# A decoder block with a mixture of experts: plain float32 down products for two of four batches, the router's weight parts side by side, and other orders on every engine

## The reference

```python
x = _layernorm(x + _L0_attn_ref(x, ...))             # a diagonal complex recurrence over the tokens
x = _layernorm(x + _L0_xattn_ref(x, fside, ctx))     # a gated product per batch, with int8 quantization
x = _layernorm(x + _L0_ffn_ref(x, gup, dp, router))  # 8 experts of width 176, the best 2 of each token
```

```python
logits = h @ router_w.T
probs = jax.nn.softmax(logits.astype(jnp.float32), axis=-1)
vals, idx = lax.top_k(probs, TOP_K)
vals = vals / vals.sum(axis=-1, keepdims=True)
combine = jnp.zeros((T, E)).at[jnp.arange(T)[:, None], idx].add(vals)
def step(acc, per_expert):
    gup, dp, cw = per_expert
    gate, up = jnp.split(h @ gup.T, 2, axis=-1)
    y = jax.nn.silu(gate) * up @ dp.T
    return (acc + cw[:, None] * y, None)
```

## Time and profile before

| | |
|---|---|
| median of 3 runs | 167.23 us (167.18, 167.23 and one of 250.56) |
| the profiled execution | 168.11 us |
| its span, first to last instruction | 166.3 us |
| PE busy | 91% |
| DVE, ACT, POOL busy | 71%, 52%, 50% |
| PE clock granted, mean | 0.987 of full |

### The profile page before, as it was taken

The page is one execution under the profiler, slowest core; times in us unless marked ns, Lnnn a source line. Parts: engine busy times, 40 slices in busy tenths (PEclk is TensorE's granted clock), DMA queues, the critical chain, the costliest instruction groups (busy, mean ns, idle before and its releaser), DMA issues.

```text
span 166.3 us, 3462 instructions
## 1 busy us (share of the span) xinstructions
PE 150.7 (91%) x1186; PEld 143.0 (86%) x1186; DVE 118.6 (71%) x395; ACT 86.0 (52%) x185; POOL 83.5 (50%) x131
## 2 busy tenths in 40 slices
PE   7599888976995999999999999999999999999980
PEld 7399666865794999899989999998999999999980
DVE  3992999989889898797998958854837725254432
ACT  7330589687872687552776645456246131522401
POOL 4710599896975039534265453323494312646412
PEclk9959999999999999999999999999999999999998
DMA  4999970000000285000444000175200015510001
GB/s 117 274 409 399 360 247 2 0 0 2 4 2 0 31 165 151 5 4 2 140 145 99 0 0 0 49 148 139 88 0 0 32 36 166 146 42 0 0 32 63
DMA packets 13313, 14.55 MB, mean 87 GB/s; under 512 B 1744, under 2 KB 13040, under 8 KB 13040
## 3 DMA queue, kind: packets, MB, share of 16 engines
q1 hardware_dynamic: 13296, 14.34, 29.1%
HBM read 13.25 MB, written 1.08 MB: 86 GB/s over the span
## 4 chain that ended last, share of the span: by engine, by line
PE 64%; DVE 16%; DMA 6%; POOL 4%; issue 3%; SPq 3%; ACT 2%; POOLq 0%; DVEq 0%; ACTq 0%
PE ps_gu L350 10%; PE ps_gu L351 10%; PE ps_gu L355 10%; PE ps_out L371 5%; PE ps_out L375 5%; PE ps_out L372 5%; DMA u_feat<-in_xT 3%; DMA gu_raw<-share_rows 2%; PE ps_gu L530 2%; DVE one_hot L1552 2%; PE ps_ab L389 1%; POOL gu_raw L1179 1%; POOL rs L1136 1%; SPq L276 1%; PE ps_ab L485 1%
## 5 line engine op out<-in xcount | busy, mean ns | idle before, releaser
L350 PE MATMUL ps_gu<-x_hi,gu_hi 128*128 128x256 f32 x176 | 47.3, 291 | 0.0
L1179 POOL TENSOR_TENSOR gu_raw<-gu_raw 128x512 f32<-128x512 f32 (+1 forms) x24 | 30.7, 1290 | 31.9 <-DVE gu_raw L1573 23.5
L351 PE MATMUL ps_gu<-x_hi,gu_lo 128*128 128x256 f32 x176 | 45.6, 282 | 0.0
L355 PE MATMUL ps_gu<-x_lo,gu_hi 128*128 128x256 f32 x176 | 35.2, 282 | 0.0
L350 PEld LDWEIGHTS ps_gu<-x_hi,gu_hi 128*128 128x128 f32 x176 | 33.1, 188 | 0.2
L351 PEld LDWEIGHTS ps_gu<-x_hi,gu_lo 128*128 128x128 f32 x176 | 33.2, 189 | 0.0
L355 PEld LDWEIGHTS ps_gu<-x_lo,gu_hi 128*128 128x128 f32 x176 | 27.0, 188 | 0.0
L1579 DVE TENSOR_TENSOR hid_lo<-gu_raw,hid_hi 128x512 fp32r<-128x512 f32 (+1 forms) x24 | 17.4, 733 | 8.9 <-ACT hid_hi L806 8.8
L1573 DVE TENSOR_TENSOR gu_raw<-sil,ps_gu 128x512 f32<-128x512 f32 (+1 forms) x24 | 15.2, 638 | 8.2 <-PE ps_gu L355 5.5
L371 PE MATMUL ps_out<-dp_hi,hid_hi 128*128 128x256 f32 x77 | 20.6, 288 | 0.3 <-DVE u_feat L1587 0.2
L788 ACT ACTIVATE sil<-ps_gu 128x512 f32<-128x512 f32 (+1 forms) x24 | 13.3, 555 | 12.8 <-PE ps_gu L355 12.7
(11 more groups left out here) (272 smaller groups left out, 318.7 us busy)
## 6 DMA issues: line engine op xcount, KB each, us to landing
gu_raw<-in_guT SPq DMA_DIRECT2D x1, 2824.0 KB, 11.7
gu_raw<-share_rows SPq DMA_DIRECT2D x16, 128.0 KB, 3.2
dp_raw<-in_dpT SPq DMA_DIRECT2D x1, 1408.0 KB, 15.1
u_feat<-in_xT SPq DMA_DIRECT2D x4, 256.0 KB, 4.4
w_feat<-in_wT SPq DMA_DIRECT2D x4, 256.0 KB, 9.5
out<-u_feat SPq DMA_DIRECT2D x8, 128.0 KB, 1.7
gu_raw<-share_rows SPq DMA_DIRECT2D x8, 112.0 KB, 3.0
gu_raw<-share_rows SPq DMA_DIRECT2D x8, 96.0 KB, 2.9
```

Of the source, the lines that this page charges most:

```text
L350: pe.matmul(dst, gu_hi[:, c, kind, col], x2_hi[:, b % 2, c], start=(c == 0), stop=False)
L351: pe.matmul(dst, gu_lo[:, c, kind, col], x2_hi[:, b % 2, c], start=False, stop=False)
L355: last = pe.matmul(dst, gu_hi[:, c, kind, col], x2_lo[:, b % 2, c], start=False, stop=(c == DC - 1))
L1179: pool.tensor_tensor(hid[:, lo:hi], hid[:, lo:hi], shares[:, lo:hi], ALU.mult).then_inc(hid_ready, 1)
```

## The change

1. For batches 0 and 1 (`b < WHOLE`, WHOLE = 2) `down` multiplies `hid` and `dp_raw` as they are, in plain float32. `hid_hi_copy` and `hid_lo_sub` exist for batches 2 and 3 only. `gated(b, p)` of batches 1 and 2 waits until the down product of the batch before has read `hid`.
2. The two parts of the router's weights lie side by side in `router_w`. A matmul with x2's high part takes both (16 columns), one with the low part takes the high weights (8); DVE adds up the two groups with a `tensor_reduce` in place of the copy. `one_hot` is one `tensor_tensor` over 128x2x2x8 in place of four `tensor_scalar`; the factor 0.5 is now in `share_copy`.
3. The phases of half the rows are a quarter turn ahead from the start (0.25 is added as they are made), so that `table` is a sine of the phase itself and an instruction of DVE with its semaphore goes. The rows of `c1` and `c2` are read in another order, from the same arrays.
4. Other orders on PE, ACT, POOL and DVE, and fewer `keep_busy` at the start.

```diff
             def down(b, t, p):
...
-                pe.wait_ge(hid_hi_ready, count_of(b, p))
-                if b == 0:
+                if b < WHOLE:
+                    pe.wait_ge(hid_ready, count_of(b, p))
+                    pe.wait_ge(l_dp, 16)
+                else:
+                    pe.wait_ge(hid_hi_ready, split_of(b, p))
+                if b == WHOLE:
                     pe.wait_ge(dpl_ready, hi // 4 + (hi % 4 > 0))
...
+                if b < WHOLE:
+                    for h in range(lo, hi):
+                        last = pe.matmul(dst, hid[:, h, tok], dp_raw[:, h], start=(h == 0), stop=(h == HC - 1))
+                else:
+                    for h in range(lo, hi):
+                        pe.matmul(dst, hid_hi[:, h, tok], dp_hi[:, h], start=(h == 0), stop=False)
+                        pe.matmul(dst, hid_hi[:, h, tok], dp_lo[:, h], start=False, stop=False)
+                    pe.wait_ge(hid_lo_ready, split_of(b, p))
+                    for h in range(lo, hi):
+                        last = pe.matmul(dst, hid_lo[:, h, tok], dp_hi[:, h], start=False, stop=(h == HC - 1))
...
                     for c in range(DC):
-                        pe.matmul(dst, x2_hi[:, b % 2, c, tok], router_hi[:, c], start=(c == 0), stop=False)
-                        pe.matmul(dst, x2_hi[:, b % 2, c, tok], router_lo[:, c], start=False, stop=False)
-                        last = pe.matmul(dst, x2_lo[:, b % 2, c, tok], router_hi[:, c], start=False, stop=(c == DC - 1))
+                        pe.matmul(dst, x2_hi[:, b % 2, c, tok], router_w[:, c], start=(c == 0), stop=False)
+                        last = pe.matmul(dst[:, 0:E], x2_lo[:, b % 2, c, tok], router_w[:, c, 0:E], start=False,
+                                         stop=(c == DC - 1))
...
-                for i in range(2):
-                    for t in range(TT):
-                        last = dve.tensor_scalar(one_hot[:, i, t], expert_no[:], top_at[:, t, i:i + 1], 0.5,
-                                                 ALU.is_equal, ALU.mult)
-                then(last)
+                then(dve.tensor_tensor(one_hot[:], expert_no[:].unsqueeze(1).unsqueeze(1).broadcast_to([P, 2, TT, E]),
+                                       top_at[:, :, 0:2].rearrange("p t i -> p i t").unsqueeze(3).broadcast_to(
+                                           [P, 2, TT, E]), ALU.is_equal))
...
             def gated(b, p):
...
-                if b > 0:
+                if b > WHOLE:
 
-                    dve.wait_ge(hid_lo_ready, count_of(b - 1, p))
+                    dve.wait_ge(hid_lo_ready, split_of(b - 1, p))
+                elif b > 0 and p < NP - 1:
+
+                    dve.wait_ge(down_done, (b - 1) * (NP - 1) + p + 1)
+                elif b > 0:
+                    dve.wait_ge(moe_done, TT * b)
...
-                then(dve.tensor_scalar(cyc[:, 0], times[:], column(11), None, ALU.mult))
+                then(dve.tensor_scalar(cyc[:, 0], times[:], column(11), signs[:, 0:1], ALU.mult, ALU.add))
...
-                dve.wait_ge(phase_ready, 1)
-
-                dve.scalar_tensor_tensor(cyc[:, 4], phase, signs[:, 0:1], phase, ALU.mult,
-                                         ALU.max).then_inc(angle_ready, 1)
```

510 lines of the change are left out of this document (239 added, 271 removed).

## The result

The changed kernel takes 169.75 us (median of 20 runs, 169.02 to 171.04). The kernel before, with the three runs shown ahead of the prediction and 17 more, takes 168.68; those three alone had given 167.23. The ratio is 1.007, with a 95% interval from 1.0048 to 1.0092: slightly slower, within 2%, and outside the range of 163.2 to 168.8. The profiled execution took 169.79 us with a span of 168.0 (before 168.11 and 166.3), so 1.7 us more are to be found.

What follows compares the result with a forecast made beforehand. PE's own work was taken to bound the kernel behind the first gate-up, with ACT, POOL and DVE full from 22 to 31 us. Terms -3.0 +3.9 -1.8 +1.1 -2.0 +0.3 = -1.5 on 167.23 gave 165.7 us; range 163.2 to 168.8.

Steps and rivals of the forecast that it cites:

- Part 5: The front, up to the first gate-up product: four steps, together -3.0 us, with -1.0 and -5.0 as bounds.
- (a): PE's start: without twelve fillers the first batch's statistics start at 13.0 us instead of 15.6, -2.6 us.
- (b): ACT's weight copies, waiting for the landing at 17.8 us, precede smooth_x(0,0): only -1.6 of the 2.6 us left.
- (c): From 22 to 31 us, one copy or instruction each on ACT, POOL and DVE leaves the chain's way: -1.0 us.
- (d): Batch 1's weights wq_r no longer stand between x2 and the first gate-up; quant_x(1) does instead: -0.4 us.
- front lost again: Rival: the chain meets the same full ACT, first gate-up moves by only 1 us; 167.7 us, chance 0.12.
- the one on the clock: Rival: PE's clock falls ahead of the first gate-up, 3.4 us of work at half clock; 167.4 us, chance 0.08.
- Part 1: Down products on PE: 44 go from three matmuls (0.34 us) to one plain float32 product (0.43): +3.9 us.
- Part 2: Router on PE: 12 matmuls a batch become 8, 16 columns costing no more: -1.8 us.
- Part 3: Ten transposes on PE move from ahead of the first gate-up to behind it, 0.11 us each: +1.1 us.
- Part 4: PE's wait for the routing before share_transpose(0) goes, -2.0 us; new waits in the new order, +0.3 us.

Runs made afterwards that it cites:

- after_plain_c: Changed kernel with the rows of c1 and c2 stored in the wanted order, each loaded as one plain block of 128 rows; 166.11 us.
- after_plain_c_four_hot: after_plain_c with one_hot again as four instructions with the factor 0.5 in them; 168.29 us.
- late_down_mended: late_down_parts with the late parts of the down weights moved into other holes on ACT and POOL; 167.97 us.
- pool_first: after_plain_c with smoothing(0) and rstd1(1) ahead of router_rest() on POOL; 166.12 us.
- before_no_fillers: Kernel before without the twelve fillers around the residual products, these in the order of batches 1, 0; ratio 1.0007.
- late_down_parts: after_plain_c with batch 0's chain ahead of weight copies, those copies spread, and down-weight parts moved to batch 1's gate-up products; 168.15 us.
- before_two_blocks: Kernel before with c1 and c2 loaded by a pattern of two outer blocks of 64 rows, same values; 173.57 us.
- before_plain_products: Kernel before with plain float32 down products for batches 0 and 1 on PE alone, wrong sums there; 171.39 us.

## Why the prediction was wrong, step by step

**What failed: the loads, priced at nothing.** Part 5, step (a) says that "PE's wait for x of batch 1, which lands at 7.91, covers it: 0", and the list of parts does not hold the change of the two loads at all. I took a landing time from before, although the transfer stands in a queue behind the one edited line, and with it the landing of the weights at 17.8 for step (b). Undoing that line gives 3.6 us (3.3 by the ratios), adding it to the kernel before costs 4.9.

**The front, (a) to (d): -3.0 expected, +2.4 measured, -0.6 with the loads mended.** (a) gave at least what it said: with plain loads the statistics start at 11.84, 3.8 us earlier than 15.64, where I had 2.6; against 13.60, which the kernel before's start gives where the clock doesn't fall, it is 1.8. (b) had the right mechanism, ACT's copies behind the landing of the weights, but took the landing as fixed. In after_plain_c they land 12.7 us behind their issue instead of 11.7, ACT's copies start at 18.81 instead of 17.8, and smooth_x gained 0.74 us (21.25) instead of 1.6. In kernels with the same plain loads it was from 11.6 to 12.7; what makes the difference isn't shown. POOL's smoothing(0), which I had overlooked, was behind the same landing, but freeing it alone left smooth_x 2.4 us behind the start of ACT's copies. (c) and (d), -1.4 together, are nowhere: from smooth_x to the first gate-up it took 21.8 us before and 21.9 in after_plain_c, where PE's clock was at 0.50 from 23.0 to 26.4 us. In after_plain_c_four_hot, the same front without the fall, it took 21.0; so they gave 0.8, and the clock took 0.9. The rival "front lost again" (167.7) and the one on the clock (167.4) describe what the mended kernel does better than my forecast. That its time of 166.11 lies near the 165.7 is luck: the front gave 2.4 us less than I wrote and the part behind it 2.4 us more.

**Part 1, +3.9: measured +3.0 to +3.5.** The step that was mis-sized is the price of the three parts, 0.34 us from one row of four blocks. Adding up, in the timeline of the kernel before, the time from each down matmul to the next start gives 31.5 us for 88 blocks, 0.36 each. The 0.43 was right, but it is made of two things: 17.7 us for 44 products, 0.40 each, and 0.19 us more for the gate-up matmul that follows a plain product (0.31 instead of 0.12 us, seven times).

**Part 2, -1.8: right.** Summed in the same way, the router takes 3.4 us instead of 5.2. Sixteen columns cost no more than eight.

**Part 3, +1.1: right.** The transposes of wq_r, tokens and the scales take 1.2 us more behind the first gate-up.

**Part 4, -2.0 and +0.3: measured -2.4 in all**, with the wait of 2.03 us and two of 0.2 gone, and no new one. The reason I gave (POOL idle during the routing) is the one the runs show, though the hole fits by 0.04 us in after_plain_c, and the rule weighed there holds for the new form as well: in late_down_mended one_hot with two inputs was held for 1.47 us. The Trainium skill, "SBUF — State Buffer", section "Who interferes with whom", has a VectorE instruction with two SBUF inputs block on a GpSimd instruction that reads SBUF; gap, one_hot, apart and combine agree: where they are held, each ends within 0.06 us of a POOL instruction's end.

With +3.2 for part 1, these make +3.2 - 1.8 + 1.2 - 2.4 = +0.2 us, and -0.8 was measured. I haven't itemised the last 1.0 us; a part is that 16 instead of 19 gate-up groups follow a transpose or a router matmul, behind which the first matmul takes 0.20 us instead of 0.12.

**The base.** My sum stood on a median of three runs, 167.23, while 20 runs gave 168.68. From the profiled execution, 168.11, the same sum would have given 166.6. That is 0.9 to 1.4 us of the 4.05 by which the forecast missed.

## What to carry to other kernels

Price every transfer whose pattern is edited, however small, and then everything issued behind it on the same queue: here two loads of 128 KB in two blocks delayed every load behind them, the gate-up weights by 4 us. Where a chain is to come earlier, look on every engine for what stands ahead of it in program order, and what that waits for: taking away one of two holds gave nothing (pool_first), both gave 0.3 us, and the freed time was then lost to the next queue. Before a difference of two profiles is put down to an edit, compare the granted clock of both stage by stage: a fall that only one of them had was 0.9 us here. And before a GpSimd instruction is put into a hole, look what short VectorE instructions run beside it there: in at least six kernels here instructions of 0.2 us took from 0.7 to 1.9 us because of that.

## What the runs showed that I had not expected

- Two outer blocks in a load's pattern: DMA share 0.13 and 0.14, four 0.32, plain 0.72 and 0.97. SP's own issue of the next transfer took 2.09 us instead of 0.43.
- The granted clock fell to 0.50 behind very different stretches: PE idle for 5.5 us (changed kernel), idle most of 18 to 22 us (after_plain_c and before_no_fillers), and busy two thirds of 32 to 40 us (late_down_parts). Each lasted from 3.4 to 10.2 us (the longest in before_two_blocks), and the three that could be priced cost 0.9, 1.6 and 2.7. Executions of one front differ in whether it falls: the start had it in the profile of the kernel before (statistics at 15.64), and not in before_plain_products, which has the same front (13.60). The profiles show no fall that follows a full stretch. The wait of 2.03 us for the routing, behind which I had seen the clock stay at 1.00, does bring it down in other executions; stages of before_no_fillers (PE busy, clock, DMA share, GB/s):

```profile
52.00:53.00 1.00, 0.00 (x0) 1.00 0.00 0
53.00:54.00 1.00, 0.69 (x4) 0.69 0.00 0
54.00:55.00 1.00, 1.00 (x7) 0.50 0.00 0
55.00:56.00 1.00, 1.00 (x6) 0.50 0.04 8
```

- A plain float32 filler of 128x128 takes 0.23 us as two instructions of 0.114, twice a transpose; a gap filled by counting one instruction a filler is overrun.
- A gate-up matmul behind a plain float32 product takes 0.31 us until the next starts, behind a transpose 0.20, behind its own kind 0.12.
